# A conditioned transformer block, 16 tiles on one core: the residual's input by its own transfer, weights in halves, the first norm in PSUM, and a new order of work

## The reference

```python
def _tc_rmsnorm(x, t, gw, gb, bw, bb):
    g = (t @ gw.T + gb)[:, None, :]
    b = (t @ bw.T + bb)[:, None, :]
    inv_rms = jax.lax.rsqrt(jnp.mean(x * x, axis=-1, keepdims=True) + EPS)
    return g * x * inv_rms + b

def _attention(x, Wq, Wk, Wv, Wo):      # 16 heads of 16 channels
    attn = jnp.einsum('blhd,bmhd->bhlm', q, k) / scale
    p = jax.nn.softmax(attn, axis=-1)
    o = jnp.einsum('bhlm,bmhd->blhd', p, v).reshape(B, L, D)
    return o @ Wo.T

def _swiglu(x, gate_w, hid_w, out_w):   # 1024 hidden channels
    return jax.nn.silu(x @ gate_w.T) * (x @ hid_w.T) @ out_w.T

x1 = x + _attention(_tc_rmsnorm(x, t, g1w, ...), Wq, Wk, Wv, Wo)
y = x1 + _swiglu(_tc_rmsnorm(x1, t, g2w, ...), gate_w, hid_w, out_w)
return x + y
```

## Time and profile before

| | us |
|---|---|
| median of 3 runs | 944.69 |
| profiled execution, its own time | 942.75 |
| profiled execution, span from first to last instruction | 940.5 |
| PE busy | 898.8 |
| DVE busy | 624.5 |
| ACT busy | 552.3 |
| POOL busy | 493.3 |
| mean granted share of the TensorE clock | 0.987 |

### The profile page before, as it was taken

How to read it: one execution, slowest core, us unless ns; L and a number is a source line. 1 busy time by engine, 2 the same in 40 slices (tenths; PEclk the granted TensorE clock), 3 DMA queues, 4 the chain that set the end, 5 groups by cost and what they waited for, 6 DMA issues and landing times.

```text
span 940.5 us, 24138 instructions
## 1 busy us (share of the span) xinstructions
PE 898.8 (96%) x8988; PEld 771.4 (82%) x8988; DVE 624.5 (66%) x1067; ACT 552.3 (59%) x1255; POOL 493.3 (52%) x409
## 2 busy tenths in 40 slices
PE   5668999999999999999999999999999999999998
PEld 3456888978888898888888888888888888888887
DVE  3637668486866848677584867758476775857642
ACT  4456657565665756566575656657575665655541
POOL 4554637364563746456373644737365472735433
PEclk9879999999999999999999999999999999999999
DMA  5300102020110101011020101102010110200000
GB/s 194 102 24 23 35 25 57 2 56 22 45 34 22 56 0 56 22 45 34 19 59 0 56 22 45 34 5 73 0 54 24 45 34 0 56 0 23 2 23 23
DMA packets 25595, 34.06 MB, mean 36 GB/s; under 512 B 3296, under 2 KB 20896, under 8 KB 25440
## 3 DMA queue, kind: packets, MB, share of 16 engines
q1 hardware_dynamic: 25344, 33.59, 11.5%
q10 hardware_dynamic: 224, 0.10, 0.0%
HBM read 25.27 MB, written 8.42 MB: 36 GB/s over the span
## 4 chain that ended last, share of the span: by engine, by line
PE 88%; DVE 4%; ACT 4%; issue 3%; DMA 1%; POOL 0%; ACTq 0%; SPq 0%; DVEq 0%
PE ps L1084 9%; PE ps L1086 9%; PE ps L1085 9%; PE ps L1220 7%; PE ps L1226 7%; PE ps L1221 6%; PE ps L1236 6%; PE ps L1239 6%; PE ps L1237 6%; PE ps L1192 5%; PE ps L1207 4%; PE ps L1112 4%; PE ps L1113 3%; PE ps L1115 3%; PE ps L1182 2%
## 5 line engine op out<-in xcount | busy, mean ns | idle before, releaser
L293 POOL TENSOR_TENSOR h_lo<-h,h_hi 128x512 fp32r<-128x512 f32 x128 | 164.1, 1291 | 178.7 <-ACT h_hi L522 178.7
L299 POOL TENSOR_TENSOR probs<-probs,recip 128x512 f32<-128x512 f32 x128 | 131.8, 1045 | 48.6 <-DVE recip L829 47.1
L840 DVE SCALAR_TENSOR_TENSOR shared<-shared,ps 128x512 f32<-128x512 f32 x128 | 86.8, 678 | 97.1 <-ACT shared L517 97.1
L1084 PE MATMUL ps<-out_w_hi,h_hi 128*128 128x256 f32 x512 | 144.9, 283 | 0.0
L1086 PE MATMUL ps<-out_w_hi,h_lo 128*128 128x256 f32 x512 | 144.7, 283 | 0.0
L1085 PE MATMUL ps<-out_w_lo,h_hi 128*128 128x256 f32 x512 | 144.2, 282 | 0.0
L1220 PE MATMUL ps<-xn_hi,gate_w_hi 128*128 128x512 f32 x256 | 106.2, 415 | 2.5 <-ACT xn_hi L488 2.0
L847 DVE SCALAR_TENSOR_TENSOR h<-shared,ps 128x512 f32<-128x512 f32 x128 | 87.4, 683 | 28.9 <-PE ps L1239 23.5
L517 ACT ACTIVATE shared<-ps 128x512 f32<-128x512 f32 x128 | 76.1, 595 | 51.6 <-PE ps L1226 51.6
L532 ACT COPY probsT<-ps 128x512 f32<-128x512 f32 x128 | 69.2, 590 | 63.1 <-PE ps L1192 63.1
L1236 PE MATMUL ps<-xn_hi,hid_w_hi 128*128 128x512 f32 x256 | 106.2, 415 | 0.0
(11 more groups left out here) (92 smaller groups left out, 2008.0 us busy)
## 6 DMA issues: line engine op xcount, KB each, us to landing
x_in<-in_x SPq DMA_DIRECT2D x16, 512.0 KB, 3.4
xT_in<-in_xT SPq DMA_DIRECT2D x16, 512.0 KB, 3.3
out<-result SPq DMA_DIRECT2D x15, 512.0 KB, 3.0
inv_all<-inv_rows SPq DMA_DIRECT2D x15, 256.0 KB, 3.9
shared<-in_attT SPq DMA_DIRECT2D x1, 1024.0 KB, 7.8
shared<-in_gateT SPq DMA_DIRECT2D x1, 1024.0 KB, 9.7
shared<-in_hidT SPq DMA_DIRECT2D x1, 1024.0 KB, 4.8
shared<-in_outT SPq DMA_DIRECT2D x1, 1024.0 KB, 5.8
```

The lines of the kernel that those rows point to most:

```text
L293: nc.gpsimd.tensor_tensor(h_lo[:, j % KEPT, :], h[:, j % 2, :], h_hi[:, j % KEPT, :].bitcast(F32), ALU.subtract).then_inc(h_lo_done, 1)
L299: nc.gpsimd.tensor_tensor(own, own, recip[:, p % TOGETHER, :].unsqueeze(2).to_broadcast([P, SEQS, L]), ALU.mult).then_inc(divided, 1)
L1084: nc.tensor.matmul(dst, a_hi, b_hi, start=first, stop=False, skip_group_check=skip)
```

## The change

**Transfers.** x_res gets its own transfer from memory, with a semaphore `x_res_loaded`; `keep_input` is gone from ACT. SP reloads x_in as soon as the squares are summed, and xT_in as soon as the rows are scaled. At the start the inputs of tile 1, and x_res of tile 0, are issued ahead of the hid weights, and the out weights after the inverse of tile 1.

**Weights in halves.** High and low parts of the gate, hid and out weights are made in two calls of 1024 columns each; `w_split` now goes to 8. The first residual and the first gate wait for 8.

**The first norm in PSUM.** `scale_first_rows` writes to two PSUM banks, and DVE does gain and shift of both halves from there (`whole_norm1`). PE spreads the inverse ahead of the products for gains and shifts.

**Order.** All lists of calls are written anew. For tile 0 DVE takes the first queries, ACT the second keys and queries.

```diff
+            sp.wait_ge(ms1_done, 1)
+            sp.dma_start(x_in[:, :, :], x_t[1]).then_inc(x_loaded, 16)
+            sp.wait_ge(scaled1, 1)
+            sp.dma_start(xT_in[:, :, :], xT[1]).then_inc(xT_loaded, 16)
+            sp.dma_start(x_res[:, :, :], x_t[0]).then_inc(x_res_loaded, 16)
+
             sp.wait_ge(w_split, 2)
...
+                elif attend:
+                    if ahead:
+                        sp.wait_ge(ms1_done, t + 1)
+                        sp.dma_start(x_in[:, :, :], x_t[t + 1]).then_inc(x_loaded, 16)
+                        sp.wait_ge(scaled1, t + 1)
+                        sp.dma_start(xT_in[:, :, :], xT[t + 1]).then_inc(xT_loaded, 16)
+                    sp.wait_ge(sum_done, t)
+                    sp.dma_start(x_res[:, :, :], x_t[t]).then_inc(x_res_loaded, 16)
...
+            def low_weights(n, lo, hi, piece, half):
+                pool.wait_ge(w_hi_done, 2 * n + half + 1)
+                nc.gpsimd.tensor_tensor(lo, raw[:, piece, half * HID:(half + 1) * HID], hi.bitcast(F32),
+                                        ALU.subtract).then_inc(w_split, 1)
...
+            def whole_norm1():
+
+                for c in range(CH):
+                    scaled = ps[:, PAIR + 2 + c, :].rearrange("p (b q) -> p b q", q=L)
+                    last = nc.vector.tensor_tensor(scaled, scaled, of_sequences(0, c, 0), ALU.mult)
+                last.then_inc(gained1, 1)
+                dve.wait_ge(gained1, 1)
+                for c in range(CH):
+                    nc.vector.tensor_tensor(xn1[:, c, :].rearrange("p (b q) -> p b q", q=L),
+                                            ps[:, PAIR + 2 + c, :].rearrange("p (b q) -> p b q", q=L),
+                                            of_sequences(1, c, 0), ALU.add).then_inc((xn1_first, xn1_second)[c], 1)
...
                 if isinstance(t, int) and t == 0:
-                    dve.wait_ge(w_split, 5)
-                dve.wait_ge(x_res_done, t + 1)
+                    dve.wait_ge(w_split, 8)
+                dve.wait_ge(x_res_loaded, 16 * t + 16)
```

More of the change, by code:

```diff
@@ L946, in steady_tile @@
                 row_maxima(t, 0)
+                shift(t, 0)
+                hidden(u, 0)
                 row_maxima(t, 1)
+                shift(t, 1)
+                silu(u, 1)
                 row_maxima(t, 2)
-                hidden(u, 0)
-                shift(t, 0)
-                silu(u, 1)
-                shift(t, 1)
                 hidden(u, 1)
-                reciprocals(t, 0)
                 row_maxima(t, 3)
+                shift(t, 2)
                 silu(u, 2)
-                reciprocals(t, 1)
-                shift(t, 2)
                 hidden(u, 2)
                 shift(t, 3)
+                reciprocals(t, 0)
+                reciprocals(t, 1)
                 reciprocals(t, 2)
@@ L1021, in last_tile @@
                 shift(t, 4)
+                hidden(u, 4)
                 shift(t, 5)
@@ L1292, in first_tile @@
                 scores(t, 0)
+                project_q(0, 1)
                 project_v(0, 1)
@@ L1324, in steady_tile @@
                 gate(u, 2)
+                hid(u, 2)
                 down(u, 0)
-                hid(u, 2)
                 gate(u, 3)
+                hid(u, 3)
+                down(u, 1)
+                gate(u, 4)
                 transpose_probs(t, 0)
                 transpose_probs(t, 1)
-                hid(u, 3)
-                gate(u, 4)
                 transpose_probs(t, 2)
@@ L1379, in last_tile @@
                 transpose_probs(t, 3)
+                gate(u, 4)
+                scores(t, 1)
+                hid(u, 4)
+                gate(u, 5)
+                values_probs(t, 0)
                 down(u, 0)
-                scores(t, 1)
                 down(u, 1)
-                gate(u, 4)
-                hid(u, 4)
-                values_probs(t, 0)
-                transpose_probs(t, 4)
-                gate(u, 5)
                 down(u, 2)
-                transpose_probs(t, 5)
                 hid(u, 5)
                 gate(u, 6)
+                transpose_probs(t, 4)
+                transpose_probs(t, 5)
                 transpose_probs(t, 6)
@@ L1424, in after_last @@
                 gate(u, 6)
+                down(u, 3)
                 hid(u, 6, False)
-                down(u, 3)
                 gate(u, 7)
```

381 lines of the change are left out of this document (197 added, 184 removed).

## The result

The changed kernel takes 967.77 us (median of 4 runs, 967.12 to 969.46), the kernel before 943.73 us beside it (4 runs, 942.25 to 944.82). The ratio is 1.026, 95% interval 1.0248 to 1.0273: slower by 24 us. The direction was forecast; the size was not, since the range ended at 963 us.

What follows compares the result with a forecast made beforehand. PE was taken to bound the steady tiles (54.95 of 55.17 us busy), engine latency the first tile. 942.75 - 13.8 + 27.0 - 1.4 = 954.6 us, put at 955.5 halfway to the median's offset; range 938 to 963 us.

Steps and rivals of the forecast that it cites:

- the steady term: Steady tiles: POOL's low parts delay DVE's norm, hidden 4 and PE's value products; +1.93 us a tile, +27.0 in 14.
- nothing gives the loss back: Steady tile's second half: it follows the value products through DVE and ACT at the same distances, so the +1.93 us stays.
- the 56.6 to 57.7 us that were to show the forecast: Sign in the changed kernel's trace: the steady period between norm transposes, against 55.17 us before.
- Tile 0: First tile, up to the first gate product: less latency between engines, 65.3 instead of 79.13 us, -13.8 us.
- the 63 to 68 that were to show it: Sign in the changed kernel's trace: the first gate product in tile 0 begins at 63 to 68 us.
- the one from the first to the second value products: Tile 0 on PE: first value products at 38.5 us, second at 48, 9.5 us between them.
- The half clock was kept for the value products alone: Tile 0: PE's idle time may mean half clock (0.85 on average before); the forecast kept that only for the value products.
- The residual waited for POOL's low parts of the out weights: End of tile 0: those low parts come last on POOL and the residual waits for them, starting at 56 us.
- The last tile: PE's wait of 1.44 us for hidden 4, ahead of the first value products, gets covered by the new order: -1.4 us.
- That the norm costs nothing: Rival, steady tile: POOL's low parts come after DVE's gain and shift, +0.1 us a tile; 928.7 or 929.5 us; chance 0.12.
- That the gain gets in first: Rival, steady tile: only DVE's shift is shut out, +0.7 us a tile; 937.4 or 938.3 us; chance 0.08.
- That tile 0 gives less than half: Rival, tile 0: out weights' low parts and transfer end later than 56 us; -6 instead of -13.8, 963 us; chance 0.08.

Runs made afterwards that it cites:

- fill_wait: The changed kernel with eight filler products on PE ahead of the first value products of each steady tile; 958.16 us.
- the two edits above: The tile 0 edits of fill_first and hid_last, each made on the changed kernel with the steady tile's next norm behind hidden 4; 931.01 and 930.40 us.
- norm_from_psum: The changed kernel with the steady tile's gain and shift reading their second input from the gate's PSUM bank instead of SBUF; 929.55 us.
- fill_first: The changed kernel with the steady tile's next norm behind hidden 4 (932.08 us), plus eleven filler products in PE's idle time of tile 0; 931.01 us.
- hid_last: The changed kernel with the steady norm behind hidden 4 (932.08 us), plus POOL's first half of low hid weights behind tile 0's last division; 930.40 us.
- hid_last_fill2: The edits of fill_first and hid_last together, with eight more filler products ahead of the norm transposes of tile 0; 929.48 us.
- old_steady_fill: The changed kernel with steady tiles in the order of the kernel before, and the tile 0 edits of fill_first and hid_last; 926.55 us.
- old_steady_fill2: old_steady_fill with eight more filler products ahead of the norm transposes of tile 0; 926.26 us.

## Where the prediction was right, and why it was wrong

**The time: above the range.** 967.77 us lie above 938 to 963. The span grew by 13.1 us more than forecast: 11.3 of them in the steady tiles, 2.6 in tile 0, and 0.8 less at the end. With the steady term alone as forecast the time would have been in the range.

**What bounds the kernel: right.** Steady tiles have no slack on PE, so a wait of PE there counts 14 times. It did.

**The steady tile: mechanism right, price too low.** The place, the releaser and the cause were forecast, and the chain by its pieces: gain 1.8 us behind the scaling (measured 1.80), the second operation 0.55 behind POOL's second low part (0.55), +1.93 us a tile (57.1 against 55.17 in the tiles at full clock: +1.9). What failed is the step behind it, "nothing gives the loss back", which asked only what is late next and not what TensorE's clock does in a wait of 2 us. In seven tiles it fell to half behind the wait, as fill_wait showed: value products and gate 5 together take 4.0 to 4.1 us there instead of 2.5, and the tile 58.6 instead of 57.1 us. 14 x 1.93 + 7 x 1.5 = 37.5 of the 38.3 us. The row that should have raised the question was in sight: a tile 0 with waits runs at 0.85, a steady tile with 0.2 us of them at 1.00. The bounds of the term, +1.4 and +2.5, came from the lock alone; the mean was +2.7. So half of the periods also lie outside the 56.6 to 57.7 us that were to show the forecast.

**Tile 0: direction right, 3 us too large.** -10.65 us to the first gate (68.48) instead of -13.8, inside its bounds of -10 to -16, but 0.5 us behind the 63 to 68 that were to show it. Norm, keys, second scores and first value products came within 0.8 us. The term that was too small is the one from the first to the second value products: 9.5 us forecast, 11.5 measured. The half clock was kept for the value products alone, while queries of tile 1 (2.7 us for six products) and transposes ran at it too. That the clock and the shift beside POOL hold this stretch is seen in the profiles of the two edits above, though not in their times; the shift itself was forecast to end at 38 and ended at 39.03. The residual waited for POOL's low parts of the out weights, as forecast. In after, DVE's residual, and POOL's halves ahead of it:

```profile
58.40 1.29 DVE L948 TENSOR_TENSOR shared<-ps,x_res 128x512 f32<-128x512 f32 x2 [3.56 <-POOL out_w_lo L316]
```

```profile
53.59 4.77 POOL L316 TENSOR_TENSOR out_w_lo<-shared,out_w_hi 128x1024 fp32r<-128x1024 f32 x2 [3.54 <-ACT out_w_hi L460]
```

**The last tile: cause right, a little too small.** -2.2 us from the norm transposes of tile 14 on, with -1.4 forecast and bounds of 0 to -2. The wait of the earlier trace rows is gone, and so is another of before that the prediction did not count, ahead of the norm transposes of tile 15:

```profile
896.38 1.07 PE L1104 MATMUL ps<-consts_sb,shared 128*128 128x128 f32 x8 [0.64 <-issue]
```

**The rivals.** That the norm costs nothing was to be decided by whether a low part starts within 2 us of the scaling's end: it starts 0.04 us before it, and the rival is out. That the gain gets in first did not happen. That tile 0 gives less than half did not happen either; 963 us would have been the nearest number, for a reason that is not there.

## What to carry to other kernels

Ahead of an operation on DVE with two SBUF inputs, look at what POOL starts in the same microsecond, and at who waits behind DVE: exchanging two lines was worth 35 us. Where TensorE has no slack, price a new wait with what the clock may cost behind it, not with its length alone; some filler products in the wait show the clock's share in one run. A kernel rewritten in several places should be tried by its places: here the new tile 0 with the old steady tile beats both.

## What the hardware showed that was not expected

Waits of 2.04 us in front of 1.1 us of value products, once in 57 us of otherwise busy PE, halved the granted clock in 7 of 14 equal tiles, at a price of 1.5 us each; the same waits with eight products in them did so in none. The lock between DVE and POOL changes hands at the end of each POOL operation, though POOL's next one has already started by the profile: DVE ends 0.55 or 0.56 us after it, both times in the steady tile, at the second operation of the first norm, and in tile 0 beside a division as beside the weights' low parts, and POOL's pair in the steady tile is 0.43 us the longer for it.

Where tile 0 became faster, the clock fell later instead: five of the kernels above (norm_from_psum, fill_first, hid_last, hid_last_fill2, old_steady_fill) have full clock at the norm transposes of tile 0 and half clock soon after the first gate, and their first period takes 56.1 to 56.5 us. In the profile of old_steady_fill2, which shows no fall there, it takes 55.09.
